# GpSimd's low part of a state ahead of its sum, and causal values as one fp32 product

## The reference

```python
def _derivative(q, p, drive, coupling, bias):
    i_couple = jnp.tanh(q) @ coupling.T
    dq = q - q ** 3 / 3.0 - p + drive + i_couple + bias
    dp = EPSILON * (q + ALPHA - BETA * p)
    return (dq, dp)
# _L0_cond_ref: 512 Runge-Kutta steps of four such stages, one after the other, over the tokens; the state q of each is kept
# _L0_attn_ref: causal attention with 16 heads of 32 and rotary embedding
qkv = jnp.einsum('bse,oe->bso', x, Wqkv_w) + Wqkv_b
scores = jnp.einsum('bthd,bshd->bhts', q, k * scale) + causal_mask
attn = jax.nn.softmax(scores, axis=-1)
out = jnp.einsum('bhts,bshd->bthd', attn, v)
...
x = x + _L0_attn_ref(_L0_cond_ref(cond, cond, x, coupling, bias), Wqkv_w, Wqkv_b)
x = x + _L0_ffn_ref(_L0_cond2_ref(x, cond, ...), ...)
```

## Time and profile before

| | |
|---|---|
| time, median of 3 runs | 5246.49 us (5240.21 to 5247.35) |
| profiled execution, its own time | 5241.32 us |
| its span, first to last instruction | 5239.5 us |
| mean granted TensorE clock | 0.704 |
| PE busy | 4524.5 us (86%) |
| PEld busy | 3762.9 us (72%) |
| DVE busy | 4151.6 us (79%) |
| ACT busy | 2403.9 us (46%) |
| POOL busy | 1731.5 us (33%) |

### The profile page before, as it was taken

The page is one execution under the profiler, slowest core; times in us unless marked ns, Lnnn a source line. Parts: engine busy times, 40 slices in busy tenths (PEclk is TensorE's granted clock), DMA queues, the critical chain, the costliest instruction groups (busy, mean ns, idle before and its releaser), DMA issues. The chain is left out here.

```text
span 5239.5 us, 214955 instructions
## 1 busy us (share of the span) xinstructions
PE 4524.5 (86%) x79237; PEld 3762.9 (72%) x79237; DVE 4151.6 (79%) x25393; ACT 2403.9 (46%) x11616; POOL 1731.5 (33%) x5957
## 2 busy tenths in 40 slices
PE   6998878878888788788888676899999999689899
PEld 5896766766666676676666565787787787578787
DVE  7999999999999999999998687778777777521123
ACT  4444444444444444444444575555555555332243
POOL 2444444444444444444443332223333222100000
PEclk5555555555555555555555797999999999899999
DMA  3000010000000000000001332222222222130211
GB/s 113 20 22 2 1 35 1 5 19 1 22 2 1 22 1 2 22 1 22 2 1 27 96 104 68 77 69 89 69 89 76 85 69 81 41 136 33 82 64 41
DMA packets 229219, 224.26 MB, mean 43 GB/s; under 512 B 82108, under 2 KB 152452, under 8 KB 228488
## 3 DMA queue, kind: packets, MB, share of 16 engines
q1 hardware_dynamic: 225216, 216.38, 13.1%
q10 hardware_dynamic: 3208, 0.68, 0.1%
q0 software_dynamic: 192, 0.03, 0.0%
HBM read 160.37 MB, written 56.67 MB: 41 GB/s over the span
## 5 line engine op out<-in xcount | busy, mean ns | idle before, releaser
L451 PEld LDWEIGHTS bank<-tanh_parts,w_lo 128*128 128x128 f16 x32768 | 1040.6, 105 | 799.1 <-ACT tanh_parts L292 797.8
L292 ACT ACTIVATE tanh_parts<-ys 128x8 f16<-128x8 f32 x4096 | 858.9, 210 | 1593.5 <-DVE ys L586 1592.3
L451 PE MATMUL bank<-tanh_parts,w_lo 128*128 128x4 f16 x32768 | 1209.9, 169 | 420.4 <-ACT tanh_parts L292 306.4
L459 PE MATMUL bank<-tanh_parts,w_hi 128*128 128x8 f16 x32768 | 1191.9, 173 | 3.8 <-issue 3.8
L459 PEld LDWEIGHTS bank<-tanh_parts,w_hi 128*128 128x128 f16 x32768 | 1050.9, 104 | 3.9 <-issue 3.9
L586 DVE TENSOR_TENSOR_SCAN ys<-mix,bank 128x24 f32<-128x24 f32 x4096 | 822.0, 204 | 77.5 <-PE bank L459 6.5
L293 ACT ACTIVATE tanh_full<-ys 128x8 f32<-128x8 f32 x4096 | 804.3, 196 | 0.0
L576 DVE TENSOR_TENSOR tanh_parts<-tanh_full,tanh_parts 128x8 f16<-128x8 f32 x4096 | 646.9, 165 | 3.7 <-ACT tanh_full L293 1.3
L1379 POOL TENSOR_TENSOR t_w_qk<-t_raw_qk,t_w_qk 128x512 fp32r<-128x512 f32 x128 | 168.2, 1336 | 681.7 <-ACT t_w_qk L1543 681.7
L770 PE MATMUL t_bank<-t_x,t_w_qk 128*128 128x512 f32 x1536 | 361.5, 391 | 12.8 <-DVE t_x L1799 12.8
L770 PEld LDWEIGHTS t_bank<-t_x,t_w_qk 128*128 128x128 f32 x1536 | 290.1, 189 | 74.0 <-DVE t_x L1799 13.5
(11 more groups left out here) (209 smaller groups left out, 9502.9 us busy)
## 6 DMA issues: line engine op xcount, KB each, us to landing
t_raw_qk<-L_cond_qkv_w_dram SPq DMA_DIRECT2D x128, 256.0 KB, 3.2
t_raw_vo<-L_cond_qkv_w_dram SPq DMA_DIRECT2D x16, 1024.0 KB, 5.2
t_raw_vo<-L_cond_out_w_dram SPq DMA_DIRECT2D x16, 1024.0 KB, 5.4
n<-t_parts SPq DMA_DIRECT2D x14, 1024.0 KB, 6.6
u_t<-u_out SPq DMA_DIRECT2D x32, 256.0 KB, 2.7
u<-u_t SPq DMA_DIRECT2D x32, 256.0 KB, 2.8
swapped<-swapped_t SPq DMA_DIRECT2D x32, 256.0 KB, 3.0
g_raw<-L_cond_ffn_w_dram SPq DMA_DIRECT2D x8, 1024.0 KB, 10.0
```

Of the source, the lines that this page charges most:

```text
L292: act.activation(tanh_parts[:, u, at, :, 0], ys[:, s, at, :, 2], ACT.Tanh, scale=1.0 / SCALE).then_inc(s_th, 1)
L451: pe.matmul(sums[:, :, 2], w_lo[:, w_of, k, m * P:(m + 1) * P], tanh_parts[:, u, k, :, 0], start=(m % 2 == 0 and k == 0), stop=False, skip ...
L459: last = pe.matmul(sums[:, :, 1:3], w_hi[:, w_of, k, m * P:(m + 1) * P], tanh_parts[:, u, k], start=False, stop=(m % 2 == 1 and k == C - 1 ...
```

## The change

In GpSimd's step, `state_low` is issued before the sum `thirds`, between the second `gq` and the wait for it. In the causal attention, the turned probabilities are copied once from PSUM to SBUF in fp32 (`pt`), three heads of a round by ScalarE and the fourth by VectorE, at the end of its round; each block of values is one fp32 product of `pt` and `val`. `val` is read from `v_t` as it is, with the constant column now written by the scan's GpSimd into `v_out` and stored with the values (33 numbers a head). `val_hi`, `val_lo`, `pt_hi` and `pt_lo` are gone. Since two engines copy, the wait for a free bank is on either of two semaphores, kept in the list `freed`.

```diff
         s_now, s_factors, s_v_ones = sem("s_now"), sem("s_factors"), sem("s_v_ones")
@@ scan, SP
+            sp.wait_ge(s_v_ones, 1)
...
@@ scan, GpSimd
+            g.memset(v_out[:, :, :, DH0], 1.0).then_inc(s_v_ones, 1)
...
                 of_net = own(tt(gq[:, 1], net[:, :, :], by_third_h, ALU.mult))
+                if low is not None:
+                    state_low(t, *low)
                 after(of_net)
                 tt(thirds[:, 0], gq[:, 0], gq[:, 1], ALU.add).then_inc(s_third, 1)
-                if low is not None:
-                    state_low(t, *low)
...
@@ causal, buffers
-        v_in = sb("v_in", [P, 2, TT, D])
+        val = sb("val", [P, 2, TT, H0, DH0 + 1])
-        val_hi = sb("val_hi", [P, 2, TT, H0, DH0 + 1], F16)
-        val_lo = sb("val_lo", [P, 2, TT, H0, DH0], F16)
-        pt = [sb(f"pt_{p}", [P, 2, 4, T], F16) for p in ("hi", "lo")]
+        pt = sb("pt", [P, 2, 4, T])
...
+ACT_HEADS = 3
+        freed, by_act, by_dve = [], 0, 0
+        for head in use_of:
+            if head[0] != "row" and head[1] < ACT_HEADS:
+                by_act += 1
+                freed.append((s_freed_act, by_act))
+            else:
+                by_dve += 1
+                freed.append((s_freed_dve, by_dve))
...
@@ causal, SP
             def load_v(row):
                 if row >= 2:
-                    sp.wait_ge(s_vlo, TT * (row - 1))
+                    sp.wait_ge(s_valued, 12 * (row - 1))
...
@@ causal, TensorE
-                    of = [part[:, k % 2, j, x * P:(x + 1) * P] for part in pt]
-                    for n, (weight, value) in enumerate(((0, val_hi), (0, val_lo), (1, val_hi))):
-                        last = pe.matmul(out_bank[:, low:high if value is val_hi else high - 1], of[weight], value[:, row % 2, s, h],
...
+                    last = pe.matmul(out_bank[:, low:high], pt[:, k % 2, j, x * P:(x + 1) * P], val[:, row % 2, s, h],
+                                     start=(j == 0 and x == 0), stop=(j == 3 and x == len(blocks) - 1), skip_group_check=True)
...
@@ causal, ScalarE
-            def high(k, j):
+            def copied(k, j):
                 act.wait_ge(s_turned, use_of[k, j] + 1)
                 if j == 0 and k >= 2:
                     act.wait_ge(s_valued, k - 1)
-                act.activation(pt[0][:, k % 2, j, 0:width(k)], turn_bank[use_of[k, j] % 2][:, 0:width(k)], ACT.Copy,
-                               scale=PT_SCALE).then_inc(s_high, 1)
+                act.activation(pt[:, k % 2, j, 0:width(k)], turn_bank[use_of[k, j] % 2][:, 0:width(k)], ACT.Copy).then_inc(s_freed_act, 1)
...
@@ causal, VectorE
-            def low(k, j):
-                v.wait_ge(s_high, 4 * k + j + 1)
-                v.scalar_tensor_tensor(out=pt[1][:, k % 2, j, 0:width(k)], in0=turn_bank[use_of[k, j] % 2][:, 0:width(k)], scalar=PT_SCALE,
-                                       in1=pt[0][:, k % 2, j, 0:width(k)], op0=ALU.mult, op1=ALU.subtract).then_inc(s_freed, 1)
+            def copied(k, j):
+                v.wait_ge(s_turned, use_of[k, j] + 1)
+                if k >= 2:
+                    v.wait_ge(s_valued, k - 1)
+                v.tensor_copy(pt[:, k % 2, j, 0:width(k)], turn_bank[use_of[k, j] % 2][:, 0:width(k)]).then_inc(s_freed_dve, 1)
...
-                    if j >= 1 and 0 <= k - 1 < ROUNDS:
-                        low(k - 1, j - 1)
                 if 0 <= k - 1 < ROUNDS:
-                    low(k - 1, 3)
+                    for j in range(ACT_HEADS, 4):
+                        copied(k - 1, j)
```

More of the change, by code:

```diff
@@ L74 @@
 CHUNKS = T // CHUNK
+H0, DH0 = 16, 32
 STATE_SCALE, TURN_SCALE = 64.0, 256.0
@@ L150, in scan_phase @@
         s_dve, s_pool = sem("s_dve"), sem("s_pool")
-        s_now, s_factors = sem("s_now"), sem("s_factors")
+        s_now, s_factors, s_v_ones = sem("s_now"), sem("s_factors"), sem("s_v_ones")
         s_kept = sem("s_kept")
@@ L222, in store_qk @@
                 sp.dma_start(u_dram[:, 2 * g * B:(2 * g + 2) * B, c * CHUNK:(c + 1) * CHUNK], of).then_inc(s_u, 16)
+            sp.wait_ge(s_v_ones, 1)
             def store_v(c, pair):
                 for b in range(2):
-                    sp.dma_start(v_dram[2 * pair + b, c * CHUNK:(c + 1) * CHUNK, :], v_out[CHUNK * b:CHUNK * b + CHUNK, pair, :]).then_inc(s_u, 16)
+                    sp.dma_start(v_dram[2 * pair + b, c * CHUNK:(c + 1) * CHUNK, :], v_out[CHUNK * b:CHUNK * b + CHUNK, pair].rearrange("p h n -> p (h n)")).then_inc(s_u, 16)
             for c in range(CHUNKS - 1):
@@ L316, in take_v @@
             def take_v(pair, n, bank):
-                act.activation(v_out[:, pair, n * 2 * P:(n + 1) * 2 * P], bank[:, 0:2 * P], ACT.Copy, scale=UNSCALE).then_inc(s_free, 1)
+                heads = slice(n * H0 // 2, (n + 1) * H0 // 2)
+                act.activation(v_out[:, pair, heads, 0:DH0], bank[:, 0:2 * P].rearrange("p (h n) -> p h n", n=DH0), ACT.Copy,
+                               scale=UNSCALE).then_inc(s_free, 1)
             def take(c, g):
@@ L809, in tile_at @@
     return None
-def value_at(k):
-    row, tile = (k + AHEAD) // 12, (k + AHEAD) % 12
-    return (row, tile) if tile < TT and 0 <= row < B else None
 def causal_phase(nc, io, x_dram, u_dram, swapped_dram, v_dram, xa_dram, held):
@@ L850, in causal_phase @@
         s_ta, s_tb, s_rot, s_rhi, s_rlo = [sem("c_" + n) for n in ("ta", "tb", "rot", "rhi", "rlo")]
-        s_vhi, s_vlo, s_ones = [sem("c_" + n) for n in ("vhi", "vlo", "ones")]
         s_scored, s_peaked, s_exped = sem("c_scored"), sem("c_peaked"), sem("c_exped")
-        s_turned, s_high, s_freed = sem("c_turned"), sem("c_high"), sem("c_freed")
+        s_turned, s_freed_act, s_freed_dve = sem("c_turned"), sem("c_freed_act"), sem("c_freed_dve")
         s_valued, s_inverse, s_taken = sem("c_valued"), sem("c_inverse"), sem("c_taken")
@@ L896, in load_v @@
                 if row >= 2:
-                    sp.wait_ge(s_vlo, TT * (row - 1))
-                sp.dma_start(v_in[:, row % 2], v_dram[row].rearrange("(i p) d -> p i d", p=P)).then_inc(s_v[row % 2], 16)
+                    sp.wait_ge(s_valued, 12 * (row - 1))
+                sp.dma_start(val[:, row % 2].rearrange("p i h n -> p i (h n)"),
+                             v_dram[row].rearrange("(i p) d -> p i d", p=P)).then_inc(s_v[row % 2], 16)
             def load_x(row):
@@ L912, in _ @@
                         load_tile(t)
-                sp.wait_ge(s_freed, use_of["row", row, C - 1] + 1)
+                sp.wait_ge(*freed[use_of["row", row, C - 1]])
                 sp.dma_start(xa_dram[:, :, row, :], xb[:, :, :]).then_inc(s_out, 16)
@@ L921, in _ @@
         def _(g):
[L922 to L925, removed]
             def rotate_first(t):
@@ L989, in values @@
                         pe.wait_ge(s_taken, k)
-                    pe.wait_ge(s_vlo, row * TT + ROUND_TILES[k % 3][-1] + 1)
-                    pe.wait_ge(s_ones, 1)
+                    pe.wait_ge(s_v[row % 2], 16 * (row // 2 + 1))
                 blocks = ROUND_BLOCKS[k % 3]
@@ L1031, in _ @@
         def _(act):
[L1032 to L1037, removed]
             def rotated_high(t):
@@ L1069, in _ @@
                         exps(k, j)
-                    if 0 <= k - 1 < ROUNDS:
-                        high(k - 1, j)
+                    if 0 <= k - 1 < ROUNDS and j < ACT_HEADS:
+                        copied(k - 1, j)
         @block.vector
@@ L1122, in _ @@
             for k in range(-AHEAD, ROUNDS + 3):
-                now, value = tile_at(k), value_at(k)
+                now = tile_at(k)
                 for j in range(4):
@@ L1128, in _ @@
                         rotate_second(now)
-                    if j == 1 and value:
-                        values_low(*value)
-                    if j >= 1 and 0 <= k - 1 < ROUNDS:
-                        low(k - 1, j - 1)
                 if 0 <= k - 1 < ROUNDS:
-                    low(k - 1, 3)
+                    for j in range(ACT_HEADS, 4):
+                        copied(k - 1, j)
                 if k >= 3 and (k - 3) % 12 == 11:
@@ L2235, in program @@
     u_dram, swapped_dram = [nc.dram_tensor(n, (P, 2 * C * B, T), F32, kind="Internal").ap() for n in ("u_t", "swapped_t")]
-    v_dram = nc.dram_tensor("v_t", (B, T, D), F32, kind="Internal").ap()
+    v_dram = nc.dram_tensor("v_t", (B, T, H0 * (DH0 + 1)), F32, kind="Internal").ap()
     n1 = [dram(f"n1_{p}") for p in PARTS]
```

24 lines of the change are left out of this document (6 added, 18 removed).

## The result

The changed kernel takes 5195.4 us (median of 4 runs, 5188.5 to 5208.0) where the kernel before takes 5245.7 (5240.2 to 5247.4): ratio 0.9908, 95% interval 0.9888 to 0.9927. The forecast was 5222 us, 24 us faster; measured are 50. The profiled execution took 5189.95 us (span 5188.1). It is one of the two faster of the four runs, with a mean granted clock of 0.709, where the two slower ones, 5200.9 and 5208.0 us, have 0.707 and 0.706.

What follows compares the result with a forecast made beforehand. VectorE was taken to set the causal stage's pace, the scan a four-stage chain; scan -10, middle -11, start -8, end +5 sum to -24 us, 5222 us forecast, range 5190 to 5285.

Steps and rivals of the forecast that it cites:

- Scan, 10 us forecast: Scan of 512 steps: `states` ahead of `thirds` gives 0.02 us a step, -10 us, between 0 and -15.
- 0.00 to 0.03 us sooner: Scan, stage 1: how much earlier the next sum on VectorE comes after the move; 0.02 taken.
- The claim that `known<-net,q` would be held: Scan, VectorE: `states` in its new place holds this instruction, which loses 0.01 to 0.05 us.
- The rival that the second sum is held: Scan: sum at 1503.29 loses 0.09 us, +0.06 a step, +31 us, total +17, 5263 us; chance 0.06.
- Middle, 11 us forecast: Causal attention, 47 rounds: 297 us at clock 0.92 against 308.2, -11 us.
- I take 0.92, a little over today's 0.89: Causal middle: granted clock assumed after the change, since TensorE's idle stretches get filled.
- the stretch by four fifths: Causal middle: four fifths of the work, loads and scores, stretch with the clock, 278 us becoming 297.
- The falling clock, my first rival at 0.22: Causal middle: clock 0.84 gives everything back, 321 us; at 0.70 373 us, 5298 in all; chance 0.22.
- TensorE becomes the bound: Causal middle: VectorE falls under 219 us and stops being the bound; TensorE's clock falls then count nearly in full.
- the 0.3 us of waits: Causal middle: waits of scores for the last `probs` of the round before, 0.3 us for three rounds (0 to 1).
- Start, 8 forecast: Start of the causal stage: `turn_b` no longer stands behind `val_lo`; -8 us (-6 to -8.5).
- End, 5 forecast: End of the causal stage: 40 blocks after the last scores cost 8.5 us in place of 3; +5 (0 to +9).

Runs made afterwards that it cites:

- Experiments 5 to 7: 5: changed kernel with fp16 probabilities and values, low parts left out, 5179.1 us; 6: 5 plus seven unread products behind each block, 5190.7 us; 7: see experiment 7.
- 9: Changed kernel with two heads copied by each of ScalarE and VectorE, second execution, timed: 5181.4 us, ratio 0.9876 to the kernel before.
- 11: Changed kernel with one head copied by ScalarE and three by VectorE: 5206.6 us.
- experiment 7: Kernel before with twelve unread fp16 products behind each turning on TensorE: 5242.3 us, ratio 0.9996 to the kernel before.
- experiment 3: Kernel before with ScalarE's and VectorE's parts of the values made two rounds later: 5240.8 us in one run.

## Why the prediction came out as it did

The direction and the mechanisms were right, but the gain was 50 us, not 24: two terms of the sum were mis-sized, both too small, by 10 and 17 us. They make up the 27 us between 5222 and 5195; of the rest the end's 4 us more and the 3.5 us of scatter behind it cancel.

- *Scan, 10 us forecast, 20 in the profiled pair, 20 in the timed one (17 over all kernels).* All three lie beyond the bound of 15 that the forecast gave. I had both observations, the 0.04 us by which TensorE's high products of stage 1 were stretched and VectorE's queue that was as late, and then let the next sum come only "0.00 to 0.03 us sooner". It came 0.036 sooner, 18 us over 512 steps: VectorE's second low part, ahead of both, moved by 0.045, and the sum moved nearly as far. Both had one cause, so the chain got back nearly the whole stall. The high products are at 0.57, as said. The claim that `known<-net,q` would be held by 0.01 to 0.05 was wrong (0.15 after as before), without effect on the sum. The rival that the second sum is held didn't occur: it takes 0.20 in both.
- *Middle, 11 us forecast, 28.5 measured.* The working for full clock was right to the tenth: three rounds 17.2 forecast, 17.28 from masks to masks in the trace (5.92, 6.21 and 5.15; the first three of a row 17.10); a row's end 2.8 forecast, 2.7 (7.86 less 5.15); a block 0.213 forecast, 0.214; the whole at full clock 278 forecast. What failed is the clock: "I take 0.92, a little over today's 0.89". It was 0.97, and 1.00 but for the first three rounds. With 0.97 the same sum gives 285 us, so the clock is some 12 of the 17 us. The other 5 are the stretch by four fifths: the low clock fell in rounds that waited anyway, and cost only 1.2 us (18.29 against 17.10 for the first three rounds of a row). I had the reason in hand (idle stretches come before a fall, and they get filled) and priced it at a third of its effect. Experiments 5 to 7 show the reason from both sides. The falling clock, my first rival at 0.22, did not come: with the fp32 block the middle had 0.92 to 0.98 in all six executions. But 9 and 11 show its milder form, a clock that is late to rise, at a price of 6.5 us and of some 15.
- *Not only TensorE.* "TensorE becomes the bound" holds, 272 of 280 us, but the ring through ScalarE's copies is as long: the 0.3 us of waits that I set for three rounds stand for it. Taking TensorE's work away gives 7 us, taking the copy away too, 31.
- *How the 28.5 us split between shorter rounds and the clock is not shown.* Before, only the last three rounds are near full clock (0.99), 18.29 us. In experiment 7, whose rounds carry the filling too, three rounds at 1.00 take 18.1 us or 19.0, by their place in the row. Against 17.3 that is 0.8 to 1.7 us, 15.7 times: by this estimate 13 to 27 of the 28.5 us are shorter rounds, and the clock is what remains. In the same places of the row the kernel before took 18.33, 19.03 and 18.09 us at 0.91, and experiment 7 took 18.31, 19.04 and 18.09 at 1.00, so between those clocks it lost nothing there.
- *The range.* Its lower end, 5190, is given as scan -15, clock 1.0, end 0; these terms add up to 5193. The 5195 that was measured lies barely above it, because the scan came out beyond its bound of 15 and the middle, 28.5, near its own of 30.
- *Start, 8 forecast, 7.3 measured*, and experiment 3 gives the same 7.3 by the one wait. `swapped` was there 0.59 us after `u`, not 1 us. *End, 5 forecast, 1.1 measured*: most of the 5.5 us that the values cost more there filled waits; I had put it in the middle of 0 to 9.
- *Cost nothing*, as said: the constant column, the 33-wide rows, the new wait on `s_v_ones`, the load of `val` behind `s_valued`.

The Trainium skill, "SBUF — State Buffer", section "SBUF: two separate sides", has GpSimd and VectorE share a port pair under an exclusive lock. The runs agree and add a size: beside a `states` of four elements `known` takes 169 ns, beside one of 128x16 237 ns, with GpSimd's record at 0.26 us in both. The start of the causal stage agrees too: `turn_b`, which starts 0.59 us behind `turn_a`, takes 1.22 us in the rows above and ends 0.55 after it, where it took 0.68 alone.

## What to carry to other kernels

Work out a stretch at full clock first, then ask separately what the clock will be; where an edit filled TensorE's idle time here, the clock was full from the fourth round on or sooner in four of the six executions with fp32 blocks, and in the other two it rose in the fourth and in the sixth round, for 6.5 and some 15 us. Give the time of the rise a range of its own. When a chain's stall shows on two engines and both wait for the same instruction, expect the whole stall back, not half of it. Before calling an engine the bound, find the longest ring of waits through the others too: here it was within 7 us of TensorE's own work, and moving one copy in four from ScalarE to VectorE (9 us in full-clock rounds) was then worth no less than making TensorE's blocks eight times cheaper (7 us).

## What the runs showed of the hardware

- The granted clock of the middle followed how full TensorE was, with fp32 or fp16 values: 272 of 280 us of fp32 work 0.97, 270 of 279 with fp16 filling 0.97, 206 of 274 at 0.85, 230 of 309 at 0.89 and the same kernel filled to 265 of 308 at 0.94. It is no function of the share alone (0.93 at 187 of 248), and it can be late to rise: 0.50 over 31 us in which TensorE was busy throughout (11).
- An fp32 product with 128x128 weights and 33 columns takes the time of its two loads, 0.107 us each at 2.4 GHz, eight times that of an fp16 one (0.026), and less than three times that of the three that it replaced (0.08).
- GpSimd's records of small instructions, 0.22 to 0.27 us, are mostly not the time in which they hold VectorE: an instruction that started 0.12 us behind `states` was free, one that started 0.01 behind it lost 0.08, and beside a `states` of four elements it lost 0.01.
